# First attention: mixing matmuls with 64-wide weights, and a division in two operations instead of four

## The reference, cut to what matters

```python
h = _rmsnorm(x, ln1_w)
q = (h @ wq.T).reshape(B, T, 4, 32).transpose(0, 2, 1, 3)
k = (h @ wk.T).reshape(B, T, 2, 32).transpose(0, 2, 1, 3)
v = (h @ wv.T).reshape(B, T, 2, 32).transpose(0, 2, 1, 3)
# rotary embedding of q and k; k and v repeated for 2 query heads each
scores = jnp.einsum('bhtd,bhsd->bhts', q, k) / jnp.sqrt(32.0)
att = softmax(where(causal, scores, -1e30))
y = jnp.einsum('bhts,bhsd->bhtd', att, v).transpose(0, 2, 1, 3).reshape(B, T, C)
x = x + y @ wo.T
flat = _rmsnorm(x, ln2_w)      # then the router, top 2 of 8 experts
```

## Time and profile before

| What | Value |
|---|---|
| Three runs | 1447.16, 1448.94, 1451.83 us |
| Median | 1448.94 us |
| The profiled execution's own time | 1445.8 us |
| Its span | 1443.7 us |
| Busy: PE, DVE, ACT, POOL | 1181.3, 1029.5, 666.0, 872.6 us |
| First graph attention | up to about 290 us |
| The causal attention's pipeline (mix of group 0 to mix of group 15) | 306.81 to 533.3 us |
| Its last indirect DMA | 581.89 us |
| The first matmul of the experts | 588.25 us |

### The profile page before, as it was taken

The page is one execution under the profiler, slowest core; times in us unless marked ns, Lnnn a source line. Parts: engine busy times, 40 slices in busy tenths (PEclk is TensorE's granted clock), DMA queues, the critical chain, the costliest instruction groups (busy, mean ns, idle before and its releaser), DMA issues. The chain is left out here.

```text
span 1443.7 us, 32648 instructions
## 1 busy us (share of the span) xinstructions
PE 1181.3 (82%) x8949; PEld 987.7 (68%) x8949; DVE 1029.5 (71%) x3999; ACT 666.0 (46%) x1725; POOL 872.6 (60%) x754
## 2 busy tenths in 40 slices
PE   6999999678878871699999994778784199999996
PEld 4777676467877771588888883445453099989995
DVE  4999999989988873467667764787875345555554
ACT  5766666236676652233333331443332055545453
POOL 3577666444477667244444442167777568887887
PEclk9999999779999985799999997677766599999998
DMA  7400000000011111566666564234432245545553
GB/s 187 63 2 2 2 2 1 1 1 16 20 39 33 39 42 55 162 196 191 199 199 194 192 211 138 78 95 146 116 117 62 81 57 73 70 62 66 71 68 44
DMA packets 126252, 122.57 MB, mean 85 GB/s; under 512 B 16577, under 2 KB 108097, under 8 KB 126129
## 3 DMA queue, kind: packets, MB, share of 16 engines
q1 hardware_dynamic: 92720, 85.65, 21.3%
q0 software_dynamic: 32960, 35.36, 12.7%
q10 hardware_dynamic: 448, 0.10, 0.0%
HBM read 76.71 MB, written 44.34 MB: 84 GB/s over the span
## 5 line engine op out<-in xcount | busy, mean ns | idle before, releaser
L2842 POOL DMA_INDIRECT out<-m_yb,m_dsti x142 | 228.3, 1608 | 65.3 <-DVE m_yb L2942 26.2
L2142 POOL DMA_INDIRECT rows<-m_yb,m_dsti x135 | 129.2, 957 | 170.3 <-DVE m_dsti L2273 148.7
L1117 POOL DMA_INDIRECT dispatch<-common_v,a1r_pos x128 | 129.9, 1015 | 55.8 <-issue 35.7
L2218 ACT ACTIVATE m_sg<-psum 128x256 f32<-128x256 f32 (+3 forms) x216 | 79.6, 369 | 179.4 <-PE psum L2171 176.4
L1375 POOL DMA_INDIRECT dispatch<-g_flat,g1r_pos x128 | 128.7, 1005 | 48.5 <-issue 33.7
L2171 PE MATMUL psum<-m_xT,m_w 128*128 128x256 f32 (+3 forms) x648 | 140.3, 366 | 0.7 <-ACT m_xT L2209 0.7
L2915 ACT ACTIVATE m_hT<-psum,m_w 128x256 f32<-128x256 f32 (+1 forms) x240 | 92.7, 446 | 99.3 <-PE psum L2869 98.4
L2171 PEld LDWEIGHTS psum<-m_xT,m_w 128*128 128x128 f32 (+1 forms) x648 | 106.2, 178 | 18.3 <-ACT m_xT L2209 0.9
L2880 PE MATMUL psum<-m_w,m_hT 128*128 128x128 f32 x848 | 105.4, 276 | 5.4 <-DVE m_yb L2938 5.1
L2880 PEld LDWEIGHTS psum<-m_w,m_hT 128*128 128x128 f32 x848 | 99.8, 192 | 6.4 <-issue 4.9
L2869 PE MATMUL psum<-m_xT,m_w 128*128 128x256 f32 (+1 forms) x480 | 103.2, 358 | 1.1 <-issue 1.0
(11 more groups left out here) (313 smaller groups left out, 3124.8 us busy)
## 6 DMA issues: line engine op xcount, KB each, us to landing
m_w<-in_c_wall SPq DMA_DIRECT2D x54, 533.0 KB
ahead_w<-in_c_wall SPq DMA_DIRECT2D x18, 533.0 KB, 3.5
g1c_y<-rows SPq DMA_DIRECT2D x32, 256.0 KB, 3.4
m_xg<-dispatch SPq DMA_DIRECT2D x47, 132.0 KB
m_xg<-dispatch SPq DMA_DIRECT2D x46, 130.0 KB, 2.2
resident<-in_c_wall SPq DMA_DIRECT2D x8, 578.0 KB, 6.2
out<-x SPq DMA_DIRECT2D x16, 256.0 KB
out<-m_yb,m_dsti POOLq DMA_INDIRECT x142, 3.3
```

Of the source, the lines that this page charges most:

```text
L1117: pool.indirect_dma_start(out=dest, out_offset=bass.IndirectOffsetOnAxis(ap=self.pos[t % 2][:, k, p:p + 1], axis=0), in_=flat[:, p, :], in ...
L2142: pool.indirect_dma_start(out=rows_out, out_offset=bass.IndirectOffsetOnAxis(ap=dsti[j][:, t:t + 1], axis=0), in_=yb[j][:, t, :], in_offse ...
L2218: act.activation(sg[j % 2][0:cn, k, 0:rows], up_banks[j % 2][k][0:cn, 0:rows], ACT.Silu)\
L2842: pool.indirect_dma_start(out=out_rows, out_offset=bass.IndirectOffsetOnAxis(ap=dsti[j][:, t:t + 1], axis=0), in_=yb[j][:, t, :], in_offse ...
```

## The change: what it does

`mix` takes 64 columns of `pt` at a time, one query head, as weights, and writes to the partition half of the frame's parity f; the query head n now picks the bank. There are 16 matmuls with 64-wide weights where there were 8 with 128-wide ones; each still streams 66 columns. In PSUM the results then lie as `y` wants them, on the partition halves by frame, and `norm` is two operations of 128 partitions instead of four of 64. The signal `y_ready` counts 2 per group instead of 4. The reciprocal keeps its shape.

```diff
-    rc_ready, y_ready = sig("rc_ready"), sig("y_ready", 4)
+    rc_ready, y_ready = sig("rc_ready"), sig("y_ready", 2)
...
-                for n in range(4):
-                    fr = 4 * u + n
-                    ins = pe.matmul(O_BANKS[fr % 2][:, w * (fr // 2):w * (fr // 2) + w], pt[:, fr, :],
-                                    vs[b][:, fr, :, :].rearrange("m k d -> m (k d)"),
-                                    start=(fr < 2), stop=True, skip_group_check=True)
+                for p in range(2 * u, 2 * u + 2):
+                    for n in range(REP):
+                        for f in range(2):
+                            ins = pe.matmul(O_BANKS[n][64 * f:64 * f + 64, w * p:w * p + w], pt[:, 2 * p + f, 64 * n:64 * n + 64],
+                                            vs[b][:, 2 * p + f, :, :].rearrange("m k d -> m (k d)"),
+                                            start=(p == 0), stop=True, skip_group_check=True)
...
-            pe.wait_ge(*y_ready.now(i, 3))
+            pe.wait_ge(*y_ready.now(i, 1))
...
-            for f in range(2):
-                for n in range(REP):
-                    rows = slice(64 * n, 64 * n + 64)
-                    m = rc[rows, f, :]
-                    dve.tensor_tensor(y[64 * f:64 * f + 64, :, n, :, :],
-                                      ov[rows, f, :, 0:D1].rearrange("n (p k) d -> n p k d", k=KV1),
+            for n in range(REP):
+                m = rc[:, n, :]
+                dve.tensor_tensor(y[:, :, n, :, :], ov[:, n, :, 0:D1].rearrange("n (p k) d -> n p k d", k=KV1),
```

More of the change, by code:

```diff
@@ L1946, in norm @@
             dve.wait_ge(*pe_yT.before(i))
-            for f in range(2):
-                for n in range(REP):
-                    rows = slice(64 * n, 64 * n + 64)
-                    m = rc[rows, f, :]
-                    dve.tensor_tensor(y[64 * f:64 * f + 64, :, n, :, :],
-                                      ov[rows, f, :, 0:D1].rearrange("n (p k) d -> n p k d", k=KV1),
-                                      bass.AP(m.tensor, m.offset, [m.ap[0], [KV1, PG], [1, KV1], [0, D1]]), ALU.mult)\
-                       .then_inc(y_ready.sem, 1)
+            for n in range(REP):
+                m = rc[:, n, :]
+                dve.tensor_tensor(y[:, :, n, :, :], ov[:, n, :, 0:D1].rearrange("n (p k) d -> n p k d", k=KV1),
+                                  bass.AP(m.tensor, m.offset, [m.ap[0], [KV1, PG], [1, KV1], [0, D1]]), ALU.mult)\
+                   .then_inc(y_ready.sem, 1)
         def out_x2(i):
```

## The result

The changed kernel took 1431.56 us (median of 6 runs, 1421.86 to 1435.11), the kernel before 1448.05 us in the same comparison (6 runs, 1443.69 to 1451.83). The ratio is 0.9877, with a 95% interval of 0.9852 to 0.9903: faster by 1.2%, 14 to 21 us, where the prediction had 6.7 us.

What follows compares the result with a forecast made beforehand. PE and ACT were taken to lead short steps, DVE three long ones, slow clock some others, with POOL's gate at the end. 2.7 + 3.6 + 0.45 = 6.7 us off 1448.94 gave 1442.2 us, range 1435.5 to 1449.

Steps and rivals of the forecast that it cites:

- Division, duration: In norm on DVE, two divisions at 0.445 us replace four, making norm 0.89 us shorter, 16 times.
- the bound that I did not take: For the new divisions on DVE: 0.355 us apiece, as a_r, making norm 1.07 us shorter.
- Where that lands: Division's saving in the attention steps: all of it in three DVE-led steps, 2.7 us, nothing in other steps.
- Mixing at full clock: On PE, mix falls from 1.90 to 1.2 us, but gains nothing because the copies of k cover it.
- Mixing at half clock: In six slow mixes on PE, scores then waits only for k: 0.05 to 1.1 us each, 3.6 us together.
- The clock falls less often: Rival: shorter PE waits before mix in DVE-led steps remove three of six falls, another 5.5 us, 1436.5 us; chance 0.09.
- The rival with more slow clock: PE idles longer before scores in short steps, so the clock falls more, 1.85 us each: 1456 us; chance 0.08.
- The dear 64-wide matmuls: Rival: in mix each 64-wide instruction costs as much as a 128-wide one, 3.8 us at full clock: 1479 us; chance 0.04.
- The end: At the last gate before the experts, 0.45 us of norm's saving comes through to POOL.
- What would show it: Signs in the changed profile: division, mix and step times, PE's and DVE's waits, and POOL's gate near 519.
- The gate near 519: POOL's last root in the attention moves from 525.64 to about 519; 10 us or more would refute the mechanism.

Runs made afterwards that it cites:

- the clock held up: Six unread matmuls per group before turned_T, added to either kernel or its halves; kernel before so filled: 1438.35 us, changed kernel so filled: 1433.20 us.
- mixing-only kernel: Kernel before with 64-wide mix, four divisions without a move between halves, and six unread matmuls per group: 1438.92 us, ratio 0.9936.
- first pair of profiles: One profile each of the unchanged kernel before and the changed kernel: POOL's gate at 525.64 and 511.57 us; profiled again, 525.66 and 509.19.

## Why the prediction was wrong in size

The sign was right, the size too small by a factor of two and more, and it was too small because two terms of the sum were reasoned wrongly. Step by step:

- *Division, duration.* Right, a little low: 1.02 us per group instead of 0.89. Back to back the new operations come 0.34 us apart, near the 0.355 of the bound that I did not take.
- *Where that lands: this is a step that failed.* "In the three DVE-led ones all of it ... 2.7 us ... In the steps to 5, 7, 12 and 15 the loop of PE and ACT leads: nothing", and nothing in the step to 9. With the clock held up the division was worth 6.4 us (both kernels with 64-wide mix, 517.43 to 510.99) to 7.6 us (both with 128-wide), in the six steps up to 13, among them those to 5, 7 and 9. There were six choices of experts in front of `norm` up to there, and I counted five. I read who led a step from its last wait (`a_r`, a_v, the rows) in steps whose length a fall had set, and took that as a sign that DVE had room in them: at full clock the wait for `a_r` is DVE's in all six. And I never asked who waits for `y` itself; the earlier trace rows has only the later wait. In the profiled pair, with falls in both kernels, the steps to 5, 7 and 15 gave 0.98, 0.85 and 1.90 us, the step to 9 0.57.
- *Mixing at full clock.* Duration right (1.15 us, forecast 1.2, from the earlier trace rows). "At full clock nowhere" holds within 0.5 us from group 3 to the gate, where both kernels have the new division (173.11 and 172.65 us). The 2.06 us of the mixing-only kernel come with divisions that are shorter too (1.55 us for 1.78).
- *Mixing at half clock, 3.6 us: the second step that failed.* I priced a fall by what `mix` lasts beyond k, and assumed that the falls stay. In the changed kernel the mixes behind group 0 that a fall touched took 1.62 to 1.98 us, and `scores` was no longer caught at half speed in full. The clock's share is 5.6 us at the gate of the first pair of profiles, 8.0 by the second. That the falls would shrink was the rival "The clock falls less often", which I gave 0.09 and 5.5 us. Its size was near, but not its ground: it expected falls to go because DVE-led steps wait less before `mix`, while with the new mix alone the falls were nearly as many as before (five for six) but a half or a third as long. And it comes on top of the division's larger gain and takes the place of the 3.6 us: 8.5 + 5.6 = 14.1.
- *The rival with more slow clock.* Its argument, more waiting on PE in every short step and so more falls, is refuted: PE waits 1.33 us instead of 0.68 in front of `scores`, and the low stretches were both shorter and fewer. The dear 64-wide matmuls are refuted by the 1.15 us.
- *The end.* The squares cover `norm` there now (1.17 us of wait before `pin`), and the stretch behind the gate lasted as before, both as forecast.
- *What would show it.* The 0.42 us divisions, 13.5 us short steps, the wait before `scores` (1.33 us, forecast 1.4) and before `pin` (1.44 us, forecast 1.6) were all seen; the waits for `a_r` "shorter by some 0.9 us each" were not. The gate near 519 was the test that failed, and the text had named that: a move of 10 us or more. Because the clock stretches changed too, the text would call this wrong in size only; the steps to 5, 7 and 9 show that where the division lands was wrong as well.

The Trainium skill, TensorEngine Tiling (Array Packing), Key Properties, speaks of a drain at each change of mode. The changed kernel has two such changes per step: the weight loads were idle 0.17 us before `mix`, as in the earlier trace rows, and the wait of 1.33 us that follows covers that. No step here is seen to get longer by it.

## What to carry to other kernels

For an operation that gets shorter, list the waits of everything that reads its result, and not only the last wait of the step; a step counts as covered only if each of these waits is ended by another. If the granted clock falls in some steps, judge who leads from steps at full clock, because a fall makes a loaded engine look idle enough. Compare gates, or any single stretch, only after one kernel has been profiled twice: here that alone moved it by 2.4 us. And price a fall by all that it takes in: in the step to 15 it was 2.45 us of `scores` and transposes, against 0.05 us of `mix`.

## What the hardware did that I had not expected

- Unread matmuls made the kernel before faster by 0.7% (0.9900 to 0.9961): 0.81 us of bf16 matmuls per step in PE's wait, and the granted clock from 290 to 526 us rose from 0.90 to 0.98.
- Work of one purpose in another form changed the clock: with 16 matmuls of 64-wide weights in place of 8 of 128-wide ones, falls were mostly 3.4 us long and not 6.8. In the 6.8 us stretches of the kernel before PE is busy all the time (6.80 of 6.80 us at 430.00); in the 3.4 us ones it is busy 2.67 of 3.40 us at 392.00 in the changed kernel, and 3.42 of 3.42 us at 320.04 in the kernel with each mix twice.
- fp32 matmul instructions with 64-wide weights and 66 columns, which alternate between the partition halves, come 36 ns apart in `mix` (1.15 us for 32), those with 128-wide weights 119 ns (1.90 us for 16). Halving the width and doubling the count made `mix` 0.75 us shorter.
- A division of 256 elements per partition takes as long on 64 partitions as on 128 (422 and 419 ns), and where it moves values between the partition halves it costs more: four in a row 1.78 us with the move, 1.55 without, and four on 128 partitions 1.42.
